# Stack rows six partitions apart, ones by a DMA, and another order of the opening loads in four attention layers

## The reference

```python
# layers 0, 1, 3 (with a mask of the batch, a mask and an adjacency, one mask for all)
scores = einsum('bhqd,bhkd->bhqk', Q, K) / sqrt(16)   # layer 1: + adj
scores = where(masked, very_negative, scores)
x = x + (softmax(scores) @ V).merge_heads() @ wo + bo
# layer 2: causal, with relative positions
scores = (QK + skew(Q @ Er.T)) / sqrt(16)
x = x + (softmax(scores) @ V).merge_heads()
```

## Time and profile before

| | us |
|---|---|
| median of 3 runs | 4222.14 (4220.96 to 4225.9) |
| the profiled execution | 4223.41, its span 4221.6 |
| TensorE busy | 3467.5 (82%) |
| DVE busy | 2559.1 (61%) |
| ACT busy | 1757.5 (42%) |
| POOL busy | 1148.2 (27%) |
| masked attention, layer 0, begins | 16.8 |
| layer 1, begins | 1067.1 |
| layer 2, begins | 2209.6 |
| layer 3, begins | 3067.7 |

### The profile page before, as it was taken

The page is one execution under the profiler, slowest core; times in us unless marked ns, Lnnn a source line. Parts: engine busy times, 40 slices in busy tenths (PEclk is TensorE's granted clock), DMA queues, the critical chain, the costliest instruction groups (busy, mean ns, idle before and its releaser), DMA issues. The chain is left out here.

```text
span 4221.6 us, 68373 instructions
## 1 busy us (share of the span) xinstructions
PE 3467.5 (82%) x18628; PEld 1741.0 (41%) x18821; DVE 2559.1 (61%) x7436; ACT 1757.5 (42%) x2506; POOL 1148.2 (27%) x1239
## 2 busy tenths in 40 slices
PE   3999999798289899995995888787349999995797
PEld 1343333344133333433663555555213434435465
DVE  4665666577477777774213776777856656654531
ACT  0454545444034444452213665666515545551111
POOL 3334341000444544420102332321231122101132
PEclk8999999899699999997997998999569999995799
DMA  5543351000434544401007998999044323403143
GB/s 112 81 76 60 63 82 26 21 1 0 92 71 85 88 86 86 81 31 47 0 14 183 284 286 248 279 298 292 9 68 56 41 37 47 55 2 110 50 102 68
DMA packets 211866, 392.80 MB, mean 93 GB/s; under 512 B 24624, under 2 KB 76688, under 8 KB 211360
## 3 DMA queue, kind: packets, MB, share of 16 engines
q1 hardware_dynamic: 168480, 296.09, 34.4%
q10 hardware_dynamic: 36864, 83.90, 5.6%
q0 software_dynamic: 6144, 8.39, 1.2%
HBM read 189.88 MB, written 96.47 MB: 68 GB/s over the span
## 5 line engine op out<-in xcount | busy, mean ns | idle before, releaser
L424 DVE CUSTOM_DVE_ANT_0 A_sums<-A_p_ps,A_bias 128x512 bf16<-128x512 f32 x1536 | 1005.7, 687 | 408.1 <-PE A_p_ps L270 386.8
L497 ACT ACTIVATE A_probs<-A_p_ps 128x1024 f32<-128x1024 f32 x640 | 653.7, 1023 | 618.2 <-PE A_p_ps L289 605.8
L270 PE MATMUL A_p_ps<-A_k_stack,A_q_stack 96*128 96x512 bf16 x1536 | 511.2, 389 | 106.3 <-DVE A_nmax L424 96.1
L284 PE MATMUL A_p_ps<-A_q_stack,A_k_stack 99*128 99x512 bf16 x1536 | 462.4, 382 | 0.1
L299 PE MATMUL A_oT_ps<-A_probs,A_v_aug 128*17 128x512 f32 x3072 | 405.2, 599 | 3.2 <-ACT A_probs L497 2.4
L270 PEld LDWEIGHTS A_p_ps<-A_k_stack,A_q_stack 96*128 96x128 bf16 x1536 | 135.6, 98 | 485.0 <-DVE A_nmax L424 387.4
L990 PE MATMUL A_t_ps<-ident,A_scores 128*128 128x128 f32 x1280 | 209.3, 298 | 118.7 <-DVE A_probsT L1072 103.5
L1082 DVE CUSTOM_DVE_ANT_0 A_scores<-A_qk_ps,A_rel_in 128x384 f32<-128x384 f32 (+3 forms) x512 | 231.9, 485 | 93.4 <-PE A_qk_ps L967 86.9
L289 PE MATMUL A_p_ps<-A_biasT,ident_bf 128*128 128x512 bf16 x910 | 282.9, 381 | 6.8 <-issue 0.4
L1072 DVE COPY A_probsT<-A_t_ps 128x1024 f32<-128x1024 f32 (+3 forms) x256 | 210.5, 822 | 110.2 <-PE A_t_ps L990 101.7
L497 ACT ACTIVATE A_probs<-A_probs 128x1024 f32<-128x1024 f32 x128 | 135.3, 1057 | 314.4 <-DVE A_probs L439 314.4
(11 more groups left out here) (355 smaller groups left out, 5862.6 us busy)
## 6 DMA issues: line engine op xcount, KB each, us to landing
A_k_stack<-A_parts SPq DMA_DIRECT2D x192, 256.0 KB, 8.9
A_q_stack<-A_parts SPq DMA_DIRECT2D x192, 256.0 KB, 9.3
A_rel_dram<-A_rel_out ACTq DMA_DIRECT2D x64, 512.0 KB, 5.6
A_rel_in<-A_rel_dram SPq DMA_DIRECT2D x64, 512.0 KB
A_rel_dram<-A_rel_out ACTq DMA_DIRECT2D x64, 384.0 KB, 6.1
A_rel_in<-A_rel_dram SPq DMA_DIRECT2D x64, 384.0 KB, 5.5
A_ctxT<-in_ctxT SPq DMA_DIRECT2D x32, 512.0 KB, 12.7
A_mask_in<-in_mask SPq DMA_DIRECT2D x64, 256.0 KB, 3.4
```

Of the source, the lines that this page charges most:

```text
L270: nc.tensor.matmul(p1_ps[i % 2][:, :], q_stack[0:KS, a_par, j * GH + i, t * P:(t + 1) * P], k_stack[0:KS, a_par, j * GH + i, :], start=Tru ...
L284: last = nc.tensor.matmul(p2_ps[half][:, i % 2, :], k_stack[:, par, j * GH + i, kb * P:(kb + 1) * P], q_stack[:, par, j * GH + i, :], star ...
L424: nc.vector.tensor_tensor_reduce(out=sums[:, i % NX, :], in0=p1_ps[i % 2][:, :], in1=bias[:, t, :], scale=-1.0, scalar=3.4028235e38, op0=A ...
L497: nc.scalar.activation(dst, src, ACT.Exp).then_inc(exp_done, 1)
```

## The change

Four edits. (1) In both attentions, and for the stacked relative table, slot s of a stack goes to partitions s, s+6, s+12 and so on, in place of 16s to 16s+15. (2) The ones of `k_stack` come from one DMA of 3 rows that reads a row of ones, which POOL sets; TensorE waits for it after frame -1. (3) SP loads masks 4 and 5 ahead of the stacks. (4) DVE makes batch 1's statistics right after the opening projections, and POOL its rstd right after mask 4. In layer 3, DVE waits for four masks ahead of frame -1, and TensorE for eight ahead of frame 0.

```diff
+        ones_row = sb("ones_row", [3, S], BF16)
...
+        def opening(b):
+            return isinstance(b, int) and b < 0
...
-                if has(b + 2, 0) and p == 7:
+                if has(b + 2, 0) and p == 7 and not opening(b):
                     dve_norm_input(dve, b + 2)
...
-                if s == 4 and then:
+                if s == 4 and then and not opening(b):
                     pool_norm(pool, b + 2)
...
-                sp.dma_start(stack[slot * HD:(slot + 1) * HD, par, :, :],
+                sp.dma_start(stack[slot:KS:SLOTS, par, :, :],
                              parts[:, which, order[slot], :, :]).then_inc(stack_ready[which], 16)
...
-            for k in range(2, TPB):
+            sp.wait_ge(ones_set, 3)
+            sp.dma_start(k_stack[KS:KS + 3, :, :, :].rearrange("r a h n -> r (a h) n"),
+                         ones_row[:, :].rearrange("r (a n) -> r a n", a=1).to_broadcast([3, 2 * H, S])).then_inc(key_ones, 16)
+            for k in range(2, TPB + 2):
                 sp_mask(sp, 0, k)
             sp_stack(sp, 0, 0, 1)
             sp_stack(sp, 0, 0, 0)
-            for k in range(TPB, MK):
+            for k in range(TPB + 2, MK):
                 sp_mask(sp, 0, k)
...
             nc.gpsimd.memset(minus_half[:, :, :], -0.5).then_inc(ones_set, 1)
+            nc.gpsimd.memset(ones_row[:, :], 1.0).then_inc(ones_set, 1)
             nc.gpsimd.memset(v_aug[:, :, :, :, HD:HD + 1], 1.0).then_inc(ones_set, 1)
-            pool.wait_ge(ones_set, 2)
+            pool.wait_ge(ones_set, 3)
             pool_norm(pool, 0)
...
                 pool_mask(pool, 0, k)
+                if k == TPB:
+                    pool_norm(pool, 1)
...
-            pe.wait_ge(ones_set, 2)
-            pe.wait_ge(key_ones, 8)
+            pe.wait_ge(ones_set, 3)
             pe.wait_ge(oT_zeroed, 1)
             pe_positions(pe, -1, 1, range(START, HALVES), plan_of(-1))
+            pe.wait_ge(key_ones, 16)
+            if not every_mask:
+                pe.wait_ge(bias_ready, MK)
...
-            for n in range(8):
-                rows = k_stack[KS:KS + 3, n // 4, n % 4 * 4:n % 4 * 4 + 4, :]
-                nc.vector.memset(rows, 1.0).then_inc(key_ones, 1)
+            dve_norm_input(dve, 1)
             if not every_mask:
-                dve.wait_ge(bias_ready, MK)
+                dve.wait_ge(bias_ready, TPB)
...
# relative_attention
-                sp.dma_start(stack[slot * HD:(slot + 1) * HD, par, :, :],
+                sp.dma_start(stack[slot:KS:SLOTS, par, :, :],
...
-                sp.dma_start(er_stack[slot * HD:(slot + 1) * HD, :], er_parts[:, K_PARTS[slot], :]).then_inc(er_ready, 16)
+                sp.dma_start(er_stack[slot:KS:SLOTS, :], er_parts[:, K_PARTS[slot], :]).then_inc(er_ready, 16)
```

## The result

The changed kernel takes 4103.74 us, the median of 4 runs (4103.41 to 4106.45); the kernel before 4221.55 (4214.47 to 4225.9, 4 runs). The ratio is 0.9724, 95% interval 0.9707 to 0.9741. The profiled execution of the changed kernel took 4103.83 us, its span 4102.1, so 119.5 us less than the span before.

What follows compares the result with a forecast made beforehand. In masked layers TensorE was taken as the bound, so gains came only where it stands still, at the heads. 25.8 + 41.7 + 26.2 + 11.5 + 7 = 112.2 us off 4223.4 gave 4111 us, range 4088 to 4142.

Steps and rivals of the forecast that it cites:

- Stack transfer: Stack DMAs of 256 KB with rows six apart: 1.2 us each in place of 2.43, bounds 0.63 and 2.43.
- k0 of batch 1: Batch 1's first k projection in each layer's head: its earlier start, 25.8, 41.7, 11.5 and 26.2 us, is the layer's gain.
- contention term: Layer 1's opening: POOL's mask 4 beside DVE's last splits delays the end of the projections by 1.5 us, bounds 0 and 4.
- What comes last: Masked heads: batch 1's context, behind mask 7's load on SP, comes last; TensorE waits 1 to 9 us for it.
- The tie in layer 1: Layer 1: POOL's late split of k0 is ready about when q0 can be evicted; loss taken as 0, 8 the other end.
- Behind k0 by engine pace: Heads: maxima, q0 and first scores follow k0 at engine pace, so the shift of k0 is the layer's whole gain.
- Ones and variance: Masked heads: removing DVE's memsets (17.1 us) alone gains nothing in layers 0 and 1; early variance lets POOL take rstd at once.
- Layer 2's steady part: Layer 2's frames: faster stack DMAs shorten the queue for skewed-score loads; 7 us, bounds 0 and 38.
- Masked frames: Steady masked layers: gain 0, as stacks are issued half a frame ahead of use and TensorE has no room.
- (B): Rival: spread rows don't speed the stacks up, only the order counts; gain 60 us, 4163 us, chance 0.10.
- (C): Rival: the strided destination hands a transfer to fewer DMA engines, so stacks get slower; about 7000 us, chance 0.02.
- (D): Rival: batch 1's earlier start exposes a wait on frame 0, half the gain goes back; 4167 us, chance 0.02.

Runs made afterwards that it cites:

- split ahead of mask 7: The "context first" kernel with, in layer 1, POOL's splits of batch 1's k ahead of the parts and conversion of mask 7; 4096.02 us.
- context first: The changed kernel with SP issuing batch 1's context right behind the stacks, ahead of masks 6 and 7; 4094.33 us.
- order alone: The changed kernel with neighbouring stack rows again, all other edits kept; 4161.26 us.
- ones alone: The kernel before with the ones made by a DMA in place of DVE memsets, nothing else changed; 4230.26 us in one run.
- ones by DVE: The changed kernel with the eight DVE memsets of ones back, ahead of batch 1's statistics, in place of the ones' DMA; 4147.94 us.
- spacing alone: The kernel before with only the stack rows spaced six apart; 4150.23 us.

## Why the prediction was right, point by point

It forecast 4111 (4088 to 4142); 4103.74 was measured. In the profiled spans 119.5 us were gained, 112.2 forecast. Part of the nearness is luck: 7 us of the gain at k0 were lost again ahead of frame 0, while layer 2's frames gave 5 us more than forecast and the masked frames 10 us that were priced at nothing.

**Stack transfer.** 1.2 us each was forecast; the six of a masked layer take 7.0 us, 1.17 each. The base was mis-sized: 2.43 us came from the stretch up to POOL's start on the mask at 67.33, but the DMA records have the twelve transfers from 38.81 to 64.95, without a pause; the rest is the mask's own load and landing. Six take 12.7 us, 2.1 each. So 0.95 us is saved on each, not 1.23. In the heads this hardly showed, because the wait behind the stacks was what counted.

**k0 of batch 1.** Forecast gains of 25.8, 41.7, 11.5 and 26.2 us in layers 0 to 3; measured 29.6, 37.6, 14.2 and 23.8. The sums are 105.2 and 105.2. That they meet is partly luck; the four misses have names:

- Layers 0 and 3 miss by +3.8 and -2.4, and the projections end 3.6 us earlier in layer 0 and 3.7 later in layer 3. No edit did that. It is TensorE's clock: a product of the opening takes 1.98 us at the full clock (2.4 GHz) and 3.75 at half of it (1.2 GHz), and how many of them run at half differs from one kernel to the next. The second k product of layer 3, in the changed kernel and then in "split ahead of mask 7", whose opening is the same (the first q product went the same way, 3.64 and 1.95). The granted clock in these two stretches is 0.50 and 1.00:

```profile
2987.43 3.78 PE L229 MATMUL A_front_ps<-A_ctxT,A_wk 128*128 128x512 f32 x4 [0.84 <-ACT A_qk L474]
```

```profile
2975.20 1.98 PE L229 MATMUL A_front_ps<-A_ctxT,A_wk 128*128 128x512 f32 x4 [0.84 <-ACT A_qk L474]
```

- Layer 1 misses by -4.1. The projections end 5.4 us late where the prediction's contention term had 1.5 (bounds 0 and 4). 3.0 are the DVE splits beside POOL, 1.8 one product more at half clock (3.78 us where it was 1.98); 0.6 stay open. The term had the right cause and half its size: two or three operations were counted, but ten of the sixteen on the timeline take longer than their shortest form (0.43 us for a cast, 0.69 for a subtraction). A second such place was missed: `dve_apply_norm` took 3.82 us beside POOL's parts (1.38 in the kernel before's opening); there the context covers it.
- Layer 2 misses by +2.7. Of the 13.3-us wait 12.6 went, where 11.5 was forecast (the other 0.7 is ACT's eviction, which comes last now), and the opening was 1.6 us shorter, by the clock again.

**What comes last.** The context of batch 1, as forecast: TensorE waits 1.1 and 6.1 us for it in layers 0 and 1, and "context first" takes the waits away. The tie in layer 1, priced at 0, held: POOL had split k0 by about 1108.2, the eviction of q0 started at 1111.72 behind its own product. "Context first" showed how near it was.

**Behind k0 by engine pace.** This step was wrong in layer 0: of 29.6 us at k0, 25.2 are left at frame 0. k0 and the two q products take 3.75, 3.52 and 3.17 us where they took 2.70, 2.99 and 1.88: 2.9 of the 4.4 us are in these three products, run wholly or mostly at half clock. Why these run at half clock isn't explained here. In layer 1, 2.2 us were lost behind k0 and in layer 3 0.8; batch 1's two k and two q products took 1.2 and 0.6 us longer there.

**Ones and variance.** Removing the memsets alone is worth nothing in layers 0 and 1: shown, by one run. What the text doesn't give is their price once the rstd isn't queued behind the masks, about 44 us; it stood in the sum only as "statistics 48.5 to 50.8". The ones' DMA was priced at one issue of SP; it also made masks 2 and 3 late (POOL's waits grew by 6.6 us), for which no run gives a price by itself.

**Layer 2's steady part.** 7 us forecast (0 to 38), 12.4 measured in one pair of profiles, and one pair can't size it. The frames of layer 2 took 705.2, 705.7 and 707.5 us in the three kernels with neighbouring rows (before, order alone, ones alone). They took 680.2 to 695.6 us in the eight with rows six apart, though these eight have the same layer 2. The longest of the eight is 10 us below the shortest of the three, and the medians, 691.6 and 705.7, are 14 us apart. So the term was about half of what the spacing gives. The stretch of the ones by DVE, to be read against that of the changed kernel (692.90 us) in the section on the result:

```profile
2238.90:2919.10 680.20, 545.63 (x5231) 356.10 (x5229) 485.39 (x1476) 436.80 (x829) 191.97 (x361) 0.93 0.86 280
```

With the same instructions TensorE is busy 554 and 546 us, at a granted clock of 0.92 and 0.93. Among the profiles at a mean clock of 0.92, the spacing gives 10 to 15 us. That the frames would change by no more than 5 us each holds.

**Masked frames.** Priced at 0; 2.6 to 4.2 us came in each layer. Layer 1's rest, 732.3 us before, is 728.7 in the changed kernel, 728.8 with spacing alone, 729.3 with order alone and 732.9 with the ones by DVE. It doesn't follow the spacing (728.8 and 729.3 with and without), nor the early variance. It scatters by as much as was gained (up to 735.6 in other runs, at a granted clock of 0.98 where the short ones have 0.99); 0 stands.

The rivals: (B), that only the order counts, is refuted by 57.5 us, and its own price was right. (C) is refuted by the landings. (D) half the gain given back: 7 us of 105 were.

## What to carry to other kernels

Here a transfer into few partitions was paid by how many of its rows crowd into the same small groups of partitions. If the consumer doesn't care which partition holds which row, spreading the rows with a stride is a change of one index, and it is to be checked slot by slot, since one stride can be good for some partitions and poor for others. At the head of a stage, price an edit by what would be late next: the same memsets were worth nothing alone and about 44 us once the queue behind them was mended, and each wait taken away uncovered another within 1 to 6 us. And compare a stretch of unchanged code over several profiles before crediting it with a gain: here identical code differed by 15 us.

## What was not expected of the hardware

- TensorE's granted clock differs between executions of the same code: layer 2's frames, where the engine is busy 80% of the time, took 680 to 696 us at a mean of 0.93 to 0.92, and the total of one kernel ran from 4075.04 (clock 0.931) to 4104.1 (0.924).
- Sixteen rows two apart in 32 partitions drain six transfers in 7.4 us, three apart in 48 partitions in 8.7, six apart in 96 in 7.0, neighbours in 12.7. Of the three-apart transfers, those into partitions 0 to 47 moved 142 GB/s and those into 48 to 95 232 GB/s.
- Behind one DMA that writes three rows of ones, SP took 8.17 us for six stack issues in place of 4.88; for 2 us the DMA share was 0.18.
- Beside a busy POOL a DVE subtraction of 128x512 took 1.63 us in place of 0.69, the normalization of a batch 3.82 in place of 1.38.
